# Moving every fourth pair's times-B product of a selective scan from VectorE to GpSimd, and folding the attention mask into the bias table

## The reference, cut to what matters

```python
def step(h, inp):                       # one step of the scan; 128 channels, 16 states, 256 steps
    dt, bt, ct, ut = inp
    h = jnp.exp(dt[..., None] * A) * h + (dt * ut)[..., None] * bt[:, None, :]
    return (h, jnp.einsum('bdn,bn->bd', h, ct))
...
delta = jax.nn.softplus(dts + dt_b[:, None, :, None])
ys = jax.vmap(_selective_scan)(xs, delta, A, Bst, Cst, Ds)     # 4 directions
y = ys.sum(0)
```

## Time and profile before

| what | value |
|---|---|
| time, median of 3 runs | 340.89 us (339.46 to 342.68) |
| span of the profiled execution | 344.4 us |
| granted TensorE clock, mean over the span | 0.857 |
| scan stage, from the first scan to the end of the last sum | 37.3 to 159.1 us |

### The profile page before, as it was taken

The page is one execution under the profiler, slowest core; times in us unless marked ns, Lnnn a source line. Parts: engine busy times, 40 slices in busy tenths (PEclk is TensorE's granted clock), DMA queues, the critical chain, the costliest instruction groups (busy, mean ns, idle before and its releaser), DMA issues.

```text
span 344.4 us, 4760 instructions
## 1 busy us (share of the span) xinstructions
PE 279.1 (81%) x1632; PEld 139.5 (41%) x1632; DVE 249.1 (72%) x654; ACT 152.3 (44%) x339; POOL 128.5 (37%) x97
## 2 busy tenths in 40 slices
PE   7998675665469589699899689999988999699692
PEld 3433111111111134113455357775546554556461
DVE  2228899999999997986775745645767465876854
ACT  1058534434424422432657345857641647224240
POOL 4003467796898986782400023420000000102002
PEclk9999559889956965858999757999999999769898
DMA  6980000000000000003100000000000000000000
GB/s 210 347 332 1 0 3 0 0 0 3 0 0 1 2 0 0 0 2 135 49 2 0 3 1 0 2 3 2 0 0 3 1 2 0 0 3 0 10 0 8
DMA packets 5289, 9.67 MB, mean 28 GB/s; under 512 B 2721, under 2 KB 3425, under 8 KB 5010
## 3 DMA queue, kind: packets, MB, share of 16 engines
q1 hardware_dynamic: 5266, 9.37, 7.9%
HBM read 9.24 MB, written 0.13 MB: 27 GB/s over the span
## 4 chain that ended last, share of the span: by engine, by line
PE 57%; DVE 29%; issue 8%; ACT 3%; POOL 2%; DVEq 0%; POOLq 0%; ACTq 0%
DVE arena L1391 10%; PE ps L811 6%; PE ps L912 6%; PE ps L897 5%; DVE arena L1378 5%; PE ps L1154 4%; PE ps L703 4%; PE ps L841 4%; DVE x L1519 3%; PE ps L1052 2%; PE ps L742 2%; PE ps L1065 2%; PE ps L709 2%; PE ps L1038 2%; PE ps L927 2%
## 5 line engine op out<-in xcount | busy, mean ns | idle before, releaser
L452 POOL TENSOR_TENSOR arena<-arena 128x1024 f32<-128x1024 f32 x31 | 77.0, 2484 | 26.0 <-DVE arena L1391 23.7
L811 PE MATMUL ps<-arena 32*128 32x510 f32 x128 | 49.8, 862 | 35.5 <-DVE arena L1378 34.0
L1391 DVE TENSOR_TENSOR_SCAN arena<-ps,arena 128x1024 f32<-128x1024 f32 x32 | 73.1, 2284 | 1.7 <-ACT ps L536 1.6
L536 ACT ACTIVATE ps<-ps,aneg 128x510 f32<-128x510 f32 x64 | 39.6, 656 | 73.4 <-PE ps L811 73.4
L817 PE MATMUL ps<-arena 32*128 32x512 f32 x128 | 49.8, 864 | 1.3 <-DVE arena L1378 1.3
L416 POOL TENSOR_TENSOR rstd<-ve,mhalf 128x2 f32<-128x2 f32 (+1 forms) x14 | 10.6, 756 | 107.1 <-DVE ve L1255 98.3
L1378 DVE TENSOR_TENSOR arena<-ps,arena 128x1024 f32<-128x1024 f32 x32 | 39.0, 1217 | 5.8 <-PE ps L817 5.4
L811 PEld LDWEIGHTS ps<-arena 32*128 32x128 f32 x128 | 12.8, 240 | 66.8 <-DVE arena L1378 47.0
L581 ACT ACTIVATE arena<-ps,cols 128x256 f32<-128x256 f32 x64 | 25.5, 473 | 14.0 <-PE ps L899 13.3
L1519 DVE SCALAR_TENSOR_TENSOR x<-ps,ww,x 128x64 f32<-128x64 f32 x88 | 18.2, 277 | 9.1 <-PE ps L927 8.9
L841 PE MATMUL ps<-arena,c 128*32 128x512 f32 x128 | 24.6, 829 | 0.0
(11 more groups left out here) (217 smaller groups left out, 539.6 us busy)
## 6 DMA issues: line engine op xcount, KB each, us to landing
arena<-in_w SPq DMA_DIRECT2D x5, 512.0 KB, 5.2
bias<-in_rpb SPq DMA_DIRECT2D x1, 1408.0 KB, 7.4
...
```

The costliest lines, as they stand in the source:

```text
L452: pool.tensor_tensor(hc[:, i % HC_SLOTS], states[i % 4], c_all, ALU.mult).then_inc(hc_done, 1)
L536: act.activation(a, a, ACT.Exp, scale=aneg[:, q:q + 1]).then_inc(exp_done, 1)
L811: pe.matmul(dst, spread[rows_, m], src, start=True, stop=True).then_inc(dspread, 1)
L1391: dve.tensor_tensor_scan(h, decay_banks(i).rearrange("p s l -> p (s l)"), h, 0.0, ALU.mult, ALU.add).then_inc(scan_done, 1)
```

## The change

1. Pairs 3, 7, 11, ..., 31 (`ON_POOL`) have their times-B product on POOL, not on DVE. POOL can't read PSUM, so PE spreads the input rows of such a pair j into bank 7, one tile in iteration j-5 and one in j-4 (`stage_input`; 0 and 1 for pair 3), ACT copies each to SBUF (`stage_copy`, into `stage`, one buffer for both tiles) and POOL multiplies from there, right behind hc(j-4) (behind hc(1) for pair 3). PE's `spread_input` leaves these pairs out. DVE's scan waits for the product through `b_pool`.
2. Bank 7 is shared, so the B and C rows move from the third and fifth iteration of a direction to the fifth and sixth (`BC_AT`), and the four `bias_blocks` from iterations 22 to 25 to iterations 28 to 31.
3. The mask is laid out on the host within the bias table `rpb` (-1e30 outside the window). The 16 additions on POOL and the 176 KB of `window` in the constant table go; DVE waits for the table's transfer instead.

```diff
+ON_POOL = [3 + 4 * n for n in range(PAIRS // 4)]
+STAGED_AT = {0: (3, 0), 1: (3, 1)}
+for _j in ON_POOL[1:]:
+    STAGED_AT[_j - 5], STAGED_AT[_j - 4] = (_j, 0), (_j, 1)
+BC_AT = (4, 5)
...
+            def times_b(j):
+                k, n = j // PAIRS_PER_DIR, ON_POOL.index(j)
+                pool.wait_ge(bc_sb, 2 * k + 1 + (k > 0))
+                pool.wait_ge(stage_sb, 2 * n + 2)
+                if j >= 4:
+                    pool.wait_ge(hc_done, j - 3)
+                b_all = bc[:, k, 0].unsqueeze(1).to_broadcast([P, 2, 2 * SEQ])
+                pool.tensor_tensor(states[j % 4], stage[:], b_all, ALU.mult).then_inc(b_pool, 1)
...
                 pool.tensor_tensor(hc[:, i % HC_SLOTS], states[i % 4], c_all, ALU.mult).then_inc(hc_done, 1)
+                if i + (2 if i == 1 else 4) in ON_POOL and i != 0:
+                    times_b(i + (2 if i == 1 else 4))
                 if i in LOST_AT:
...
-                if i in MASK_AT:
-                    mask_head(MASK_AT.index(i))
...
+            def stage_copy(j, s):
+                n = ON_POOL.index(j)
+                act.wait_ge(stage_ps, 2 * n + s + 1)
+                if n and s == 0:
+                    act.wait_ge(b_pool, n)
+                act.activation(stage[:, s], bank(7), ACT.Copy).then_inc(stage_sb, 1)
...
+                if i - 1 in STAGED_AT:
+                    stage_copy(*STAGED_AT[i - 1])
...
+            def stage_input(i):
+                j, s = STAGED_AT[i]
...
+                pe.matmul(bank(7), spread[rows_, m], dd[rows_, k, 1], start=True, stop=True).then_inc(stage_ps, 1)
...
-                if i + 1 < PAIRS:
+                feeds = i + 1 < PAIRS and i + 1 not in ON_POOL
+                if feeds:
                     delta_known(i + 1, 1)
-                    pe.wait_ge(mul_done, i + 1)
+                    pe.wait_ge(mul_done, muls(i + 1))
...
-                if k < DIRS - 1 and ii in (2, 4):
-                    bc_mm(2 * (k + 1) + (ii == 4))
-                if 22 <= i < 26:
-                    bias_blocks(i - 22)
+                if i in STAGED_AT:
+                    stage_input(i)
+                if k < DIRS - 1 and ii in BC_AT:
+                    bc_mm(2 * (k + 1) + BC_AT.index(ii))
+                if 28 <= i < 32:
+                    bias_blocks(i - 28)
...
-                if i + 1 < PAIRS:
+                if i + 1 < PAIRS and i + 1 not in ON_POOL:
                     times_b(i + 1)
...
+                if i in ON_POOL:
+                    dve.wait_ge(b_pool, ON_POOL.index(i) + 1)
+                else:
+                    dve.wait_ge(mul_done, muls(i + 1))
```

More of the change, by code:

```diff
@@ L89 @@
 DELTA_U_AT = {12: 2, 19: 3}
-MASK_AT = [9, 10, 16, 17, 18] + list(range(20, 31))
+ON_POOL = [3 + 4 * n for n in range(PAIRS // 4)]
[3 more added lines that the diff above has]
+BC_AT = (4, 5)
 LOG_FROM = 2.0 ** -6
@@ L189, in build @@
         idle = sb("idle", [P, 512], BF16)
+        stage = sb("stage", [P, 2, 512])
         log_from, log_at = sb("log_from", [P, 1]), sb("log_at", [P, 1])
@@ L360, in log1p, with muls, staged @@
             eng.tensor_tensor(z1[k], z1[k], dd[:, k, 1], ALU.add).then_inc(log1p_ready[on], 1)
+        def muls(n):
+            return n - sum(j < n for j in ON_POOL)
+        def staged(n):
+            return sum(i < n for i in STAGED_AT)
         pair_tiles = [[(2 * (i % 2) + s, (i % PAIRS_PER_DIR) // 2) for s in range(2)] for i in range(PAIRS)]
@@ L428, in _ @@
             pool.memset(w_i2[:], 0.0).then_inc(w_i2_padded, 1)
-            def mask_head(n):
-                if n == 0:
-                    pool.wait_ge(load["rpb"], 16)
-                    pool.wait_ge(load["c32"], 16)
-                q, h = divmod(n, HEADS)
-                pool.tensor_tensor(bias[:, q, h], bias[:, q, h], window[:, q], ALU.add).then_inc(bias_ready, 1)
+            def times_b(j):
[6 more added lines that the diff above has]
+                pool.tensor_tensor(states[j % 4], stage[:], b_all, ALU.mult).then_inc(b_pool, 1)
             lost(pool, 0)
@@ L569, in _ @@
                     square(LOG_AT[i])
-                if k < DIRS - 1 and ii in (3, 5):
-                    bc_copy(2 * (k + 1) + (ii == 5))
+                if i - 1 in STAGED_AT:
+                    stage_copy(*STAGED_AT[i - 1])
+                if k < DIRS - 1 and ii - 1 in BC_AT:
+                    bc_copy(2 * (k + 1) + BC_AT.index(ii - 1))
             def experts(f, im, func):
@@ L753, in bc_mm @@
                     pe.wait_ge(bc_sb, q)
+                if q >= 2:
+                    pe.wait_ge(stage_sb, staged(PAIRS_PER_DIR * (q // 2 - 1) + BC_AT[0]))
                 pe.matmul(bank(7), w_bc[:, q // 2, q % 2], u[:, 0 if q < 4 else 2], start=True, stop=True).then_inc(bc_ps, 1)
@@ L782, in bias_blocks @@
                     pe.wait_ge(bc_sb, 2 * DIRS)
+                    pe.wait_ge(stage_sb, len(STAGED_AT))
                 half = n // 2
@@ L818, in spread_input @@
                 last.then_inc(uspread, 1)
+            def stage_input(i):
+                j, s = STAGED_AT[i]
+                k = j // PAIRS_PER_DIR
+                g, m = pair_tiles[j][s]
+                rows_ = slice(32 * g, 32 * g + 32)
+                if s == 0:
+                    pe.wait_ge(*u_made(k))
+                    pe.wait_ge(bc_sb, 2 + 2 * k)
+                if staged(i):
+                    pe.wait_ge(stage_sb, staged(i))
+                pe.matmul(bank(7), spread[rows_, m], dd[rows_, k, 1], start=True, stop=True).then_inc(stage_ps, 1)
             def spread_ahead(i):
                 delta_known(i, 0)
-                if i + 1 < PAIRS:
+                feeds = i + 1 < PAIRS and i + 1 not in ON_POOL
+                if feeds:
                     delta_known(i + 1, 1)
-                    pe.wait_ge(mul_done, i + 1)
+                    pe.wait_ge(mul_done, muls(i + 1))
                 if i == 1:
@@ L1371, in times_b @@
             def times_b(i):
-                dve.wait_ge(uspread, i + 1)
+                dve.wait_ge(uspread, muls(i + 1))
                 if i % PAIRS_PER_DIR == 0:
@@ L1662, in _ @@
                 mark(dve.tensor_tensor(xb, src, pr_b, ALU.add))
-            dve.wait_ge(bias_ready, 2 * HEADS)
+            dve.wait_ge(load["rpb"], 16)
             for v in range(IMAGES * HEAD_PAIRS):
@@ L1842, in constants @@
         c["tap_sum"][i[ok], r * CH + rows[r][ok] // TAPS] = 1
-    start = np.clip(np.arange(SIDE) - WIN // 2, 0, SIDE - WIN)
-    for q in range(2):
-        qi, qj = 8 * q + i // SIDE, i % SIDE
-        key = np.arange(KEYS)
-        ki, kj = KEY_ROW0[q] + key // SIDE, key % SIDE
-        inside = ((ki[None] >= start[qi][:, None]) & (ki[None] < start[qi][:, None] + WIN)
-                  & (kj[None] >= start[qj][:, None]) & (kj[None] < start[qj][:, None] + WIN))
-        c["window"][:, q * KEYS:(q + 1) * KEYS] = np.where(inside, 0.0, -BIG)
     c["rank8"][:] = np.tile(8 - np.arange(8), TB)
@@ L1856, in constants, with in_window @@
     return np.concatenate(list(c.values()), 1), np.concatenate(list(h.values()), 1).astype(mybir.dt.np(BF16))
+def in_window(q):
+    start = np.clip(np.arange(SIDE) - WIN // 2, 0, SIDE - WIN)
+    i, key = np.arange(P), np.arange(KEYS)
+    first_i, first_j = start[8 * q + i // SIDE][:, None], start[i % SIDE][:, None]
+    ki, kj = KEY_ROW0[q] + key // SIDE, key % SIDE
+    return (ki >= first_i) & (ki < first_i + WIN) & (kj >= first_j) & (kj < first_j + WIN)
 def lay_out(a):
@@ L1902, in lay_out @@
         o["rpb"][token, q, :, at] = a["L1_conv_rpb"][:, di[near], dj[near]].T
+        o["rpb"][:, q] = np.where(in_window(q)[:, None], o["rpb"][:, q], -BIG)
     qkv, qkv_b = a["L1_conv_qkv_w"], a["L1_conv_qkv_b"]
```

9 lines of the change are left out of this document (3 added, 6 removed).

## The result

The changed kernel takes 346.94 us in the median of 20 runs (341.33 to 359.9), the kernel before, run beside it, 339.91 (20 runs, 336.34 to 348.2). Their ratio is 1.0162, with a 95% interval of 1.0122 to 1.0202: slower by 1.6%, some 5.5 us; forecast were 345 us and a ratio of 1.012.

What follows compares the result with a forecast made beforehand. DVE sets the pace from 78 to 108 us; later it partly waits for PE. Product 30's end at 146.9, plus 3 for PE and 13.6 of tail, gives 163.5 against 159.1: 340.9 + 4.4 = 345 us, range 332 to 352.

Steps and rivals of the forecast that it cites:

- DVE's own gain: Scan stage: eight products leave DVE, 1.12 us each, 9.0 us if nothing else is late.
- The `log1p` wait: Scan stage, sets 2 and 3: DVE's `delta_log` waits for POOL's `log1p`, delayed by a product; 1.6 and 2.6 us.
- Overlap of side work: Scan stage: DVE's side operations meeting a POOL instruction wait for its end, then run; 7.2 us for the rest.
- Rival (b): Scan stage: DVE's side work seldom meets POOL, only two `log1p` waits remain; 332 to 337 us, chance 0.20.
- load of over 90%: POOL in the scan stage: hc, eight products and six half-size operations make 104.5 us, leaving it nearly gapless.
- side operation ends 0.55 us after POOL's: Scan stage: a DVE side operation meeting one on POOL waits, ending some 0.55 us after it.
- PE's part in the middle: Scan stage: PE's extra work at the lower clock delays DVE; 3 us taken, bounds 0 to 7.
- rival (a): Scan stage: PE at the higher clock, port waits as forecast; about 337.6, up to 342 us; chance 0.25 with no change.
- The staged spreads don't run beside others: PE in the scan stage: 16 staged spreads each cost a two-tile spread, 1.8 us at the lower clock, half at the higher.
- The tail: End of product 30 to last sum, with late bias blocks: 13.6 us, midway between 8.9 (higher clock) and 18.2 (lower).
- the argument against the higher clock: Stage end in the kernel before: from 147.10 to 159.09 us PE is busy without a gap, yet its rate stays low.
- POOL's mask worth nothing: POOL in the scan stage: the mask's 8.9 us filled gaps spent waiting for scans, so removing them gains nothing by itself.

Runs made afterwards that it cites:

- e5: The changed kernel with `delta_log`, `delta` and `delta_u` of sets 2 and 3 one scan later; 349.8 us, ratio 1.032 to the kernel before.
- e7: The changed kernel with only pairs 23, 27 and 31 on POOL, bias blocks still late; 342.3 us, ratio 1.011 to the kernel before.
- e6: The changed kernel with POOL's products of pairs 11 and 19 behind `log1p`, not ahead of it; 350.0 us, ratio 1.018 to the kernel before.
- e3: The kernel before with the mask in the bias table and eight extra, unread products on POOL, DVE keeping all 32; 352.2 us, ratio 1.040.
- e12: e3 with POOL's eight extra products replaced by memsets that read nothing; 351.1 us, ratio 1.033 to the kernel before.
- e1: The kernel before with only the mask moved into the bias table; 338.8 us, ratio 1.005.
- e2: The kernel before with only the four bias blocks moved from iterations 22 to 25 to 28 to 31; 342.4 us, ratio 1.012.
- e10: The changed kernel with its bias blocks in iterations 16 and 17, all eight products on POOL; 344.4 us, ratio 1.014 to the kernel before.
- e4: The changed kernel with all products back on DVE, staged spreads and copies kept but unread; 344.5 us, ratio 1.017 to the kernel before.
- e9: e7 with the bias blocks in iterations 14 to 17, read behind scan 18; 340.4 us, ratio 0.988 to the kernel before.
- e11: The kernel before with only the bias blocks moved to iterations 13 to 16, read behind scan 17; 344.4 us, ratio 1.017.

## Why the prediction was right, step by step

The forecast of 345 us, 4.4 above before, met 5.5 by the ratio, in the range and on the side that had the largest chance. Counted from the first scan, the forecast stage ends at 126.2 us and measured 126.0. That this fits so well is luck. Three terms were off and cancelled: scan 20 came at 87.0 and not 81.8 (+5.2), from there to the end of product 30 it took 29.0 and not 30.8 (-1.8), and the end 10.0 and not 13.6 (-3.6). And it is the stage of one execution, after's shortest, with the short end; e5 and e7, with the same work there, took 15.4 us from product 30 on. The direction, and POOL's new place as the cost, were right for the reason given.

- **DVE's own gain**, 1.12 us for each product: right. e7 shows it free of side effects, 3.5 us for three.
- **The `log1p` wait**, 1.6 and 2.6 us, 4.2 in all: mis-sized, and the largest error. It measured 10.0: 5.9 us idle and 2 x 2.06 of stretch. Two things were left out. The walk took POOL's products as ready when hc ended, but product 11 waited 2.12 us for its staged copy. And it ended the cost when `log1p` ends; POOL starts its next hc at that moment, and DVE's `delta_log` stands behind the whole of it. e6 separates them: the idle time gone, the stretch whole.
- **Overlap of side work**, 7.2 us for the rest: 4.8 measured. `bounded_from` of set 2 cost 1.8 (forecast 1.4), set 3 before `delta_log` 1.5 (1.9); pair 3's scan waited 1.1 us for POOL's product, where the forecast had 1.8 for `delta` of set 1, and a product 0.8, where it had 1.1 for `small_log`, which itself ran 0.4 us shorter than before. All these come to 14.8 us against 11.4; with 1.1 us of waits for PE, less the 5.7 saved, that is 10.2 of the 10.8 us by which scan 20 is later. Rival (b), that they seldom meet, is ruled out by e3: POOL's load alone makes the stage 13.3 us longer. But the "load of over 90%" that spoke against (b) was not there (77% up to scan 20): POOL was late at the hand-overs without being full. The "side operation ends 0.55 us after POOL's" held for those with two inputs (`delta_log` and `small_log` in after, 0.55 each time); the TENSOR_SCALAR ones, which the forecast priced by the same rule, ended 0.28 us after it. In e12 two-input instructions pass POOL's fills at 0.67 us, while TENSOR_SCALAR is held (1.57). The Trainium skill (SBUF — State Buffer, Who interferes with whom) has it that two SBUF inputs contend only with GpSimd's reads, and that `tensor_scalar` can run in a mode that takes the shared pair whole; the runs agree with both.
- **PE's part in the middle**, 3 us between 0 and 7: at most 1.2 in after (29.0 against 27.8), but it depends on the clock. With 0.94 in this half it was what rival (a) says; e5 and e6, with the same PE work, took 37.9 and 37.0 us from scan 20 to 31 and not 34.1. "The staged spreads don't run beside others" failed in part: in after's timeline at 145.59 the staged spread (L858), delta rows and input rows run within the same 0.7 us.
- **The tail**, 13.6 between 8.9 and 18.2: 10.0 in after's profile, at a granted clock of 1.00. The low-clock end exists too: e5 and e7 take 15.4 us from product 30 on (clock 0.56), less than the 18.2. The middle of the two bounds was no case of its own. And the argument against the higher clock was misread: in before the lower clock did not hold to 159.09, it rose at 156.9, after 9.8 us of PE busy without a gap. Windows of before:

```profile
150.00:157.00 7.00, 7.00 (x26) 1.44 (x18) 5.36 (x4) 4.33 (x8) 5.13 (x4) 0.51 0.00 1
157.00:159.10 2.10, 2.09 (x10) 0.29 (x8) 1.06 (x2) 0.24 (x1) 0.00 (x0) 1.00 0.00 0
```

- **POOL's mask worth nothing**: e1 agrees (1.000 to 1.009).
- **"Behind the stage nothing changes"**: in the program, yes; in time, no. The same instructions took 179.1 to 189.1 us, and what lies ahead of the stage 32.9 to 37.3.

So one place of the loss is shown, POOL's added time ahead of scan 20: e3 costs 4.0% before the gain of 2.6% (9.0 us) is taken off, and after's own trace is 10.8 us late there. The other, the bias blocks at the end, costs 1.2% when moved alone (e2) and 3.2 us in the tail of e7's trace; that it is part of after's 1.6% is not shown. After's profiled execution has the short end, and e10, with the blocks early, is not to be told from after. e3 and e4 with the gain of eight products would make 3.1%, and 1.6% is measured, so the terms don't add (each also holds e1's 0.5%). e7 beside e2 (1.011 and 1.012, both with the blocks late) shows that three products without side work around them cost nothing in time, and gain nothing either; the per cent that e9 has rests on two runs.

Open is what sets the clock, in the stage and behind it. e3 and e12, with the longest stages, have 0.95 behind it, and e11, with the shortest, 0.89, which reads as if won time were given back; but e10, with a stage of 125.5 us, has 0.95 and e5, with 127.8, 0.92, and no run changed this alone. e9's 0.89 is of an execution 7 us above the two behind its ratio. Because of this spread e2's 1.2% and e11's 1.7% can't be placed by their traces. By the ratios after is some 3.9 us slower than e1; its stage is 5.6 us longer, but the two profiled executions are only 1.8 us apart, since after's is 2.5 us shorter ahead of the stage and 1.3 behind. That e5's long end comes from the clock is read from its windows, not tested; why the clock fell there, where after kept it, is open.
